# Two DMA transposes split in two each: high half first, low half when it is ready

## The reference, cut to what matters

```python
x = x + tanh(g_xattn[0]) * matmul(fake_quant(layernorm(x)), fake_quant(ctx))
x = x + tanh(g_ffn[0])   * (layernorm(x) @ W_base.T + b + low_rank_update)
x = x + tanh(g_xattn[1]) * attention(layernorm(x), ctx)   # 16 heads of 96, 4 key/value heads,
                                                          # keys: ctx and x, 1536 rows; then @ Wo.T
x = x + tanh(g_ffn[1])   * moe(layernorm(x))              # logits = h @ router.T (64 experts), softmax,
                                                          # top 8: h * sum(top) + top @ expert_bias
```

## Time and profile before

| | us |
|---|---|
| median of 3 runs | 1089.94 |
| lowest, highest | 1089.33, 1093.16 |
| the profiled execution, its own time | 1089.94 |
| span of the profiled execution | 1088.1 |
| PE busy in the span | 1040.1 (96%) |
| POOL, DVE, ACT busy | 645.6, 620.0, 619.4 |
| DMA transposes issued: probabilities, `turn_o`, `turn4` | 256, 31, 7 |

### The profile page before, as it was taken

One profiled execution on the slowest core, in us unless ns is written; L12 is line 12 of the kernel. 1 busy time (PEld: TensorE's weight loads), 2 busy tenths in 40 slices (PEclk: granted clock), 3 DMA queues, 4 the chain that ended last, 5 costly groups with the idle time before them and its releaser, 6 DMA issues.

```text
span 1088.1 us, 18287 instructions
## 1 busy us (share of the span) xinstructions
PE 1040.1 (96%) x7207; PEld 586.0 (54%) x7207; DVE 620.0 (57%) x1067; ACT 619.4 (57%) x687; POOL 645.6 (59%) x349
## 2 busy tenths in 40 slices
PE   8969999999999999999999999999999999989875
PEld 3535544444544555555665666666656655655542
DVE  6867949653222455555555645654654654667656
ACT  5756635432122676655666756666756567577733
POOL 4458678433000588756667856657865667678841
PEclk9989999999999999999999999999999999999996
DMA  9777664762323999999999999999999999999983
GB/s 337 249 245 216 200 223 126 165 97 53 76 74 101 207 204 212 214 204 191 202 185 205 196 196 201 182 206 195 188 223 198 177 201 173 164 187 172 182 169 116
DMA packets 521064, 198.93 MB, mean 183 GB/s; under 512 B 486468, under 2 KB 501700, under 8 KB 520980
## 3 DMA queue, kind: packets, MB, share of 16 engines
q1 hardware_dynamic: 520980, 197.77, 88.4%
HBM read 56.88 MB, written 13.63 MB: 65 GB/s over the span
## 4 chain that ended last, share of the span: by engine, by line
PE 83%; DMA 5%; DVE 4%; SPq 3%; POOL 2%; ACT 2%; issue 1%; POOLq 0%; DVEq 0%; ACTq 0%
PE ps L559 30%; PE ps L795 19%; PE ps L769 11%; PE ps L810 10%; PE ps L812 5%; PE ps L696 3%; PE ps L581 2%; POOL region_y L1698 1%; SPq L521 1%; DMA v_scratch<-region_o 1%; SPq L519 1%; DMA ln_t<-stage 1%; DMA region_c<-region_b 1%; DMA region_o<-region_y 1%; DVE p_max L1534 1%
## 5 line engine op out<-in xcount | busy, mean ns | idle before, releaser
L1698 POOL TENSOR_TENSOR region_y<-p,region_b 128x1536 f16<-128x1536 f32 x128 | 396.7, 3100 | 279.8 <-ACT region_b L1237 259.0
L1227 ACT ACTIVATE p<-ps,p_max 128x1536 f32<-128x1536 f32 x128 | 197.2, 1541 | 200.7 <-DVE p_max L1534 200.6
L1534 DVE TENSOR_REDUCE p_max<-ps 128x1 f32<-128x1536 f32 x128 | 224.9, 1757 | 131.4 <-PE ps L795 131.4
L795 PE MATMUL ps<-region_q,region_c 96*128 96x512 f16 x1152 | 269.8, 379 | 0.8 <-DMA region_c<-region_q 0.8
L810 PE MATMUL ps<-region_q,region_c 128*128 128x192 f16 x1536 | 207.6, 246 | 11.0 <-DMA region_o<-region_y 6.8
L1237 ACT ACTIVATE region_b<-ps,p_max 128x1536 f16<-128x1536 f32 x128 | 196.5, 1535 | 31.7 <-DMA region_c<-region_b 31.5
L812 PE MATMUL ps<-region_q,region_o 128*128 128x96 f16 x1536 | 202.3, 206 | 0.0
L810 PEld LDWEIGHTS ps<-region_q,region_c 128*128 128x128 f16 x1536 | 150.2, 98 | 28.3 <-issue 8.2
L795 PEld LDWEIGHTS ps<-region_q,region_c 96*128 96x128 f16 x1152 | 105.3, 98 | 108.8 <-issue 1.1
L812 PEld LDWEIGHTS ps<-region_q,region_o 128*128 128x128 f16 x1536 | 150.2, 98 | 13.6
L559 PE MATMUL ps<-region_w,region_q 128*128 128x512 f16 x576 | 135.4, 381 | 4.2 <-POOL region_w L1698 2.4
(11 more groups left out here) (147 smaller groups left out, 1111.4 us busy)
## 6 DMA issues: line engine op xcount, KB each, us to landing
stage<-ctx_in SPq DMA_DIRECT2D x16, 512.0 KB, 4.8
stage<-ctx_t_in SPq DMA_DIRECT2D x15, 512.0 KB, 6.9
stage<-wq_in SPq DMA_DIRECT2D x16, 384.0 KB, 3.9
stage<-wo_in SPq DMA_DIRECT2D x16, 384.0 KB, 4.3
k_scratch<-region_o SPq DMA_DIRECT2D x12, 384.0 KB, 5.3
region_q<-k_scratch SPq DMA_DIRECT2D x8, 576.0 KB, 5.7
region_q<-v_scratch SPq DMA_DIRECT2D x8, 576.0 KB, 6.6
x_res<-x_in SPq DMA_DIRECT2D x8, 512.0 KB, 9.4
```

The source lines that it names most:

```text
L795: ins = nc.tensor.matmul(bank(NSB * (m % 2) + sb_), q_head[0:HD, b, h, hq, qt * P:(qt + 1) * P], k_head[0:HD, b, hk, sb_ * 512:(sb_ + 1) * ...
L1227: nc.scalar.activation(p32[:, m % 2, :], rows, ACT.Exp, bias=p_max[:, m % 4:m % 4 + 1], accum_out=den[:, m % 4:m % 4 + 1]).then_inc(e32_ok, 1)
L1534: nc.vector.reduce_max(p_max[:, m % 4:m % 4 + 1], rows, axis=AX, negate=True).then_inc(max_ok, 1)
L1698: return nc.gpsimd.tensor_tensor(out, a, b, op)
```

## The change

Each of the two combined transposes becomes two: one for the high half, issued as soon as the high cast is counted, and one for the low half, issued when the low half is. Both count on the same semaphore, so everybody who waits for it waits for twice the count.

```diff
             def turn_o(k):
                 if k >= 2:
                     sp.wait_ge(wo_ready, 2 * k - 2)
-                sp.wait_ge(o_lo_ok, k + 1)
-                sp.dma_start_transpose(o_t[:, k % 2, :, :, :].rearrange("p h j q -> p (h j) q"),
-                                       o_cast[:, :, :].rearrange("p h n -> p (h n)")).then_inc(o_ld[k % 2], 16)
+                for h, ready in ((HI, o_hi_ok), (LO, o_lo_ok)):
+                    sp.wait_ge(ready, k + 1)
+                    sp.dma_start_transpose(o_t[:, k % 2, h, :, :], o_cast[:, h, :]).then_inc(o_ld[k % 2], 16)
 
             def turn4(i):
-                sp.wait_ge(y4_lo, i + 1)
-                sp.dma_start_transpose(cols(ln_t, i * HSLAB, HSLAB).rearrange("p (c k) -> p c k", c=2 * NC),
-                                       y4_cast[:, i % 2, :, :].rearrange("p h d -> p (h d)")).then_inc(turned4[i % 2], 16)
+                for h, ready in ((HI, y4_hi), (LO, y4_lo)):
+                    sp.wait_ge(ready, i + 1)
+                    sp.dma_start_transpose(slab(i, h).rearrange("p (c k) -> p c k", c=NC), y4_cast[:, i % 2, h, :]
+                                           ).then_inc(turned4[i % 2], 16)
...
-                pe.wait_ge(o_ld[k % 2], use(k, 2))
+                pe.wait_ge(o_ld[k % 2], 2 * use(k, 2))
...
-                pe.wait_ge(turned4[i % 2], use(i, 2))
+                pe.wait_ge(turned4[i % 2], 2 * use(i, 2))
...
-                    act.wait_ge(o_ld[(k - 1) % 2], use(k - 1, 2))
+                    act.wait_ge(o_ld[(k - 1) % 2], 2 * use(k - 1, 2))
...
-                    act.wait_ge(turned4[i % 2], use(i - 2, 2))
+                    act.wait_ge(turned4[i % 2], 2 * use(i - 2, 2))
```

## The result

The changed kernel takes 1097.53 us (median of 6 runs) against 1089.63 us (6 runs): a ratio of 1.0078, with a 95% interval of 1.0054 to 1.0101. It is slower by about 8 us, where 1089.1 us and a range up to 1093.5 us were forecast. Its profiled execution took 1099.59 us, span 1097.7 us, so it stands 2 us above its own median.

The account below looks back on a forecast made before the run. PE was taken as the bound, saturated from 525 to 957 us, with SP's queue as the resource spent. +0.4 + 0.6 - 1.0 - 0.7 - 0.4 + 0.3 = -0.8 on 1089.94 gave 1089.1 us, 8-in-10 range 1086.3 to 1093.5.

Parts of the forecast that it names:

- PE is the bound from 525 to 957, and only a stall can cost.: Five attention steps: PE busy 432.09 of 432.10 us, so transfers or issues cost only by making PE wait.
- The price of the issues and the landings.: SP's queue: about 1.2 us per 384-column issue, 1.23 per 1024; a 1024-column half lands 3.1 us after its start.
- The units of the odd steps without slack, 23 and 55.: Low transposes landing just as weigh needs them; two turn_o ahead, so each costs up to 2.4 us if issues add.
- As the row speaks for a full queue, I take 0.4 us in all, near the lower end.: Attention's added turn_o issues: shorter later issues give time back; 0.4 us lost, bounds 0 and 5.1.
- The fifth step's 0.4 us as an upper bound: Fifth attention step: about 2 us of slack at its tightest unit against up to 2.4 us delay, so 0.4 lost at most.
- `turn_o(0)`: First step, on SP's chain: the added issue costs 0.6 us, bounds 0 and 1.2.
- `turn4`: Last stretch: splitting gains 1.0 us at turn4(0), 0.7 at turn4(3), 0.4 at turn4(4), 0 at the others.
- `turn_o(29)`: Last stretch, on the chain: the low half goes out later, costing 0.3 us, bounds -0.5 and +0.8.
- the first rival, the issues add: Every microsecond of SP's added issue is paid where there is no slack: 1096.5 us, chance 0.09.
- point of decision: The first rival decides if the queue behind SP is empty at units 19 to 23 and 51 to 55.
- The second rival, a fixed cost on the DMA engines: Each added DMA keeps the engines for 1.8 us, stretching the saturated steps: 1102 us and more, chance 0.04.
- the signs that were named: Profile after: ln_t wait from 2.8 to about 1.1 us, shorter low issues; region_o<-region_y waits in step three or four refute.

Follow-up runs that it names:

- e9: Original kernel with turn_o split only in steps 2, 4 and 6 (12 of 31), turn4 one DMA: 1092.20 us, 1.0012 of the original.
- e10: Original kernel with turn_o split only in steps 1, 3 and 5 (12 of 31), turn4 one DMA: 1093.51 us, 1.0025 of the original.
- e1: Original kernel with turn_o alone split, turn4 one DMA: 1099.96 us, 1.0070 of the original.
- e2: Original kernel with turn4 alone split, turn_o one DMA: 1088.62 us, 0.9973 of the original.
- e18: Original kernel with 50 satisfied waits (1.54 us of SP) ahead of each unsplit turn_o, no DMA added: 1099.78 us, 1.0082 of the original.
- e5: Original kernel with 40 satisfied waits (1.23 us of SP) ahead of each unsplit turn_o, no DMA added: 1095.39 us, 1.0035 of the original.
- e17: Original kernel with 20 satisfied waits and one plain DMA of 128 partitions x 8 bytes ahead of each unsplit turn_o: 1098.10 us, 1.0057 of the original.
- e14: Original kernel with turn4 split, turn_o one DMA, Wo loads moved from units 3-6 to 9-12: 1087.94 us, 0.9972 of the original.
- e7: Original kernel with turn_o as three DMAs of 256 columns behind the low half's count, turn4 one DMA: 1129.63 us, 1.0347 of the original.
- e16: Original kernel with turn4 split, turn_o one DMA, the 12 Wo loads on ACT's queue: 1093.80 us, 1.0031 of the original.
- e15: Changed kernel (turn_o and turn4 split) with the 12 Wo loads on ACT's queue: 1102.57 us, 1.0095 of the original.

## Why the prediction was wrong

- *PE is the bound from 525 to 957, and only a stall can cost.* Right: where there was slack the split costs nothing (e9, steps 2, 4, 6).
- *The price of the issues and the landings.* Right: 1.2 us was forecast for 384 columns, 1.26 is the median; 1.23 for 1024, and landings from 2.25 against 2.3.
- *The units of the odd steps without slack, 23 and 55.* Right as places: PE waits 1.78 us at `weigh(55)` and 0.56 us at `weigh(23)`. There are others beside them, at the starts of the odd steps. That unit 23 had no slack was a misreading: its landing was put at 488.8 by adding 2.2 us to the end of a long issue, but the trace has it 5.3 us after the start, at 488.0, 0.9 us ahead of `weigh(23)`. For unit 55 the estimate was right within 0.2.
- *"As the row speaks for a full queue, I take 0.4 us in all, near the lower end."* This step failed. The odd steps lost 5.7 us, PE idle for 4.95, against an upper bound of 5.1. That an issue took 2.78 us where 1.41 would do was read as time that a later issue gives back. Before, SP's queue around unit 55 was

```profile
653.43 1.26 SPq L498 DMA_TRANSPOSE region_q<-region_q  x1
654.79 2.00 SPq L519 DMA_TRANSPOSE region_c<-region_b  x1
656.84 2.78 SPq L521 DMA_TRANSPOSE region_o<-region_y  x1
```

  so the pair of probability issues took 4.78 us; after, it took 2.58 + 1.52 = 4.10. But from the start of `turn_o(11)` (unit 51) to the end of the low issue of unit 55 SP took 29.5 us before and 31.7 after: of the 2.5 us that two `turn_o` bring in, 0.4 came back. Nor is a shorter issue an earlier landing. The low transpose of unit 55 landed 2.4 us later than before, counted from the start of step 3. The low issue of unit 23 shrank from 3.92 to 1.66 us, and that transpose landed 2.4 us later too, counted from the start of step 1. From 344 us on, the 256 probability issues did not shrink: 493 us before, 501 after. So what was to follow from a full queue did not come true where it counts; that a long issue means a full queue at all is shown by no row. The holds show the price without a DMA: 0.75 us each are free, 1.23 cost 0.35%, 1.54 0.8%, 2.44 2.6%. So there is a reserve for each `turn_o`; it ends between 0.56 and 1.11 us of SP's time as the table counts it, below the 1.40 that a split adds, and beyond it the price climbs steeply.
- *The fifth step's 0.4 us as an upper bound* (step 5 here). Too low: 1.8 us. The bound took the slack at one unit as constant and the delay as that of two `turn_o`; e10, in which step 5 loses only 0.4 us, suggests that lateness is also carried in from the step before.
- *`turn_o(0)`*: 0.6 forecast. PE's wait in unit 10, 1.6 us before, is 1.9 in the kernel after and 2.2 in e1, which fits. The length of step 0 can't decide it: it is 0.3 and 0.7 us longer in these two, but 1.2 in e2, where `turn_o` is whole.
- *`turn4`*: -2.1 us in all was forecast, -2.9 measured (e2). The mechanism is right where SP stood idle ahead of it (`turn4(3)`, and the backlog behind `turn4(4)`), and wrong for `turn4(0)`, whose wait of 2.1 us stayed at 2.0. In the changed kernel's profile the wait for `ln_t` is 2.5 us, not 1.1; 2.2 of it is that of `turn4(0)`. Nor does the gain of e2 add to the loss of e1: the changed kernel is at 1.0078, e1 at 1.0070, e1 times e2 would be 1.0043, just below the interval. The last low transpose lands 101.7 us after the start of step 7, in e2 98.9, before 99.9; and the clock fell once more.
- *`turn_o(29)`*: +0.3 forecast, its wait is 1.5 instead of 1.7 us; about zero.

What happened is the first rival, the issues add, at 1096.5 us, to which 0.09 was given; the measured 1097.5 is 1 us above. That it comes so near is in part luck: its 0.4 us for step 5 was 1.8, its 1.2 for the first step 0.3 to 0.6, and the last step, 0.8 - 0.5 in its sum, was 2.0 us longer, for the most part by the clock. Its point of decision was put wrongly: the long issues stood at those units, and the added ones were paid all the same. The chance had been set by a plausible buffer whose depth no row gave. The second rival, a fixed cost on the DMA engines, falls: e18 costs as much as the split and adds no DMA, and neither the landings nor the DMA share rose. Of the signs that were named, PE's wait for `region_o<-region_y` in steps 3 and 5 did come. The low transposes were to be issued in less time: those of units 20 to 24 were, 10.7 us in all against 13.8, those of units 51 to 56 hardly, 13.9 against 14.3.

What stays open: an added issue of 384 columns takes 1.40 us of SP on the mean, 0.2 more than its least; whether the queue behind SP does that is not known, nor how much that queue holds. Near 1.1 us the price is loosely known, 0.35% (e5) and 0.57% (e17), with intervals that overlap. What the second queue does to the transposes can't be told from the moment of issue (e15, e16). And it is open why the gain of `turn4` does not show beside a split `turn_o`. The coalescing rule of the Trainium skill, page "DMA: Bandwidth & Descriptors", section "Rules for kernel authors", had the sign for `turn_o`; for `turn4` the runs go the other way. The 2.0 us of its section on the anatomy of a DMA does not serve as a price: here the first 31 added DMAs cost 0.28 us each on average, the next 31 0.94.

The best version measured is the half of the change that gains, `turn4` alone, e2 at 0.9973 (0.9958 to 0.9987), with e14 beside it at 0.9972.

## What to carry to other kernels

When a queue is in unbroken issue ahead of a consumer without slack, count an added issue in full, and do not take a long issue as a cushion. Splitting a transfer pays where the issuing queue stands idle before the second half's data are ready, and costs where it is late already: look at each place in the timeline, as one DMA can be right in one step and wrong in the next. To price an issuing queue's time, hold it by known amounts at several doses; one dose gives a point, and here 0.75 us was free where 2.44 cost 28 us. And measure the time that an issue takes on the mean, not its least: only then did the hold and the split agree. Last, before a loss is put down to waits, look at the granted clock: after some of PE's waits it fell, and the loss grew.

## What the runs showed of the hardware that was not expected

- The response to SP's time is far from linear: 0, 0.35, 0.82 and 2.62% for 0.75, 1.23, 1.54 and 2.44 us ahead of each of 31 issues.
- How long an issue holds SP does not tell when the data land: the low transpose of unit 23 landed 5.3 us after the start of an issue of 3.92 us before, 1.4 us after its end, and 4.0 us after the start of one of 1.66 us in the kernel after, 2.4 us after its end.
- PE's clock fell to 1.2 GHz for stretches of 3.4 us in the midst of the attention, at 632.4 in e7 after a wait of 2.45 us, and six times in all there; the kernel before has none in that part, though PE waits 2.4 us once. What decides it is not shown.
- Issuing 12 loads of 384 KB on ACT's queue instead of SP's, in the same units but 12 to 19 us sooner, made the kernel 0.6% slower (e16 against e2), though SP had less to issue and the issues, 0.55 us each on ACT, ran beside its exponentials. The Trainium skill, page "DMA: Bandwidth & Descriptors", section "Issuing engines are not separate DMA queues", says that both run on the same engines and that a second issuer saves only issue time; no run here shows the engines of each queue, and the time saved at SP did not pay for what the move cost. Whether the queue or the moment cost it is open.
- Moving the Wo loads by six units moved the stalls from the early to the late units of the odd steps, whose products PE runs in the next step, with little change to their sum (5.7 us in steps 1, 3 and 5; 6.1 us in steps 2, 4 and 6).
